# A graph network on one core: gathers and scatters of the GpSimd queue without waits for tiles and links

## The reference

```
h = max(layernorm(x), 0);  x = x + L0(h, src, dst)
h = max(layernorm(x), 0);  x = x + L1(h, edge_index, theta)
h = max(layernorm(x), 0);  x = x + L2(h, ..., edge_type)
h = max(layernorm(x), 0);  x = x + L3(h, src, dst)

# L2, for each edge e with x = h[src], y = h[dst]:
c      = w_comp[etype]                            # 16 coefficients
msg    = sum over b of c[b] * (x @ weight[b])     # 16 bases of 32 x 32
x_hat  = x @ A1_w.T + A1_b
y_hat  = y @ A2_w.T + A2_b + rel_emb[etype]
a      = tanh(relu(sum(x_hat * y_hat) / sqrt(32)))
h_new  = relu(segment_sum(a * msg, dst) + self-loop)  # where a node receives

# L3:
repeat 10 times: h = 0.9 * norm * segment_sum((norm * h)[src], dst) + 0.1 * feat
```

## Time and profile before

| | |
|---|---|
| median of 3 runs | 2976.82 us (2969.91 to 2977.31) |
| the profiled execution's own time | 2974.17 us |
| its span, first to last instruction | 2972.4 us |
| granted clock of TensorE | 1.00 throughout |
| busy: POOL, DVE, PE, ACT | 66%, 58%, 14%, 11% |

### The profile page before, as it was taken

The page is one execution under the profiler, slowest core; times in us unless marked ns, Lnnn a source line. Parts: engine busy times, 40 slices in busy tenths (PEclk is TensorE's granted clock), DMA queues, the critical chain, the costliest instruction groups (busy, mean ns, idle before and its releaser), DMA issues.

```text
span 2972.4 us, 14542 instructions
## 1 busy us (share of the span) xinstructions
PE 410.3 (14%) x2009; PEld 196.7 (7%) x2009; DVE 1735.8 (58%) x2999; ACT 329.6 (11%) x1032; POOL 1951.7 (66%) x1883
## 2 busy tenths in 40 slices
PE   0000000000000000000000039806870000015000
PEld 0000000000000000000000013302320000015000
DVE  8998885666786768112866658867789311431000
ACT  0000021111001110000111024403430000000000
POOL 6576777775456770577777755473668777466776
DMA  1001022221011310101210100000001100010000
GB/s 19 14 11 25 15 58 48 47 48 26 25 41 25 133 25 17 40 11 41 48 43 20 27 9 6 2 3 5 7 7 56 57 9 8 5 42 9 8 8 5
DMA packets 71098, 78.34 MB, mean 26 GB/s; under 512 B 38122, under 2 KB 63944, under 8 KB 69752
## 3 DMA queue, kind: packets, MB, share of 16 engines
q0 software_dynamic: 59456, 23.50, 6.0%
q1 hardware_dynamic: 5720, 28.67, 2.5%
q10 hardware_dynamic: 5856, 25.60, 2.3%
HBM read 36.82 MB, written 48.69 MB: 29 GB/s over the span
## 4 chain that ended last, share of the span: by engine, by line
DVE 41%; issue 27%; POOL 15%; PE 6%; another core or an unknown queue 4%; DVEq 2%; DMA 2%; ACT 1%; POOLq 0%; ACTq 0%; SPq 0%
POOL out L1525 10%; DVE mf L491 7%; DVE pay L491 4%; DVE z L491 3%; DVE psum L888 3%; POOL xs L1519 2%; DVE psum L494 2%; DVE mf L875 2%; PE psum L1941 2%; DVE mf L870 2%; PE psum L1942 1%; DVE outs L491 1%; POOL mf L1519 1%; DVE st L515 1%
## 5 line engine op out<-in xcount | busy, mean ns | idle before, releaser
L1525 POOL DMA_INDIRECT out<-outs,i_outS x196 | 224.8, 1147 | 130.8 <-DVE z L1338 73.1
L1519 POOL DMA_INDIRECT xs<-in_x,i_src x196 | 217.2, 1108 | 134.4 <-issue 54.8
L1519 POOL DMA_INDIRECT xd<-in_x,i_dst x196 | 208.5, 1064 | 108.3 <-DVE mf L491 44.6
L1519 POOL DMA_INDIRECT xd<-x_rows,i_dstX x196 | 205.7, 1050 | 106.6 <-issue 49.8
L1519 POOL DMA_INDIRECT mf<-x_rows,i_srcX x196 | 209.1, 1067 | 95.3 <-issue 60.0
L1525 POOL DMA_INDIRECT out<-outs,i_srcX x196 | 198.9, 1015 | 71.9 <-issue 61.5
L1519 POOL DMA_INDIRECT pay<-payload_by_dst,i_rank x196 | 195.6, 998 | 62.6 <-issue 62.6
L491 DVE TENSOR_TENSOR mf<-mf 128x128 f32<-128x128 f32 (+5 forms) x577 | 175.0, 341 | 14.0 <-DVE mf L491 3.5
L491 DVE TENSOR_TENSOR pay<-psum,pay 128x512 f32<-128x512 f32 x196 | 133.4, 688 | 85.2 <-ACT pay L1826 68.4
L1519 POOL DMA_INDIRECT mf<-l_own_rows,lists x124 | 123.8, 998 | 49.7 <-issue 37.4
L1519 POOL DMA_INDIRECT mf<-l_first_rows,lists x124 | 125.2, 1010 | 37.7 <-issue 37.7
(11 more groups left out here) (465 smaller groups left out, 2384.2 us busy)
## 6 DMA issues: line engine op xcount, KB each, us to landing
z<-in_x ACTq DMA_DIRECT2D x16, 624.0 KB
out<-z ACTq DMA_DIRECT2D x16, 624.0 KB
l_first_rows<-mf SPq DMA_DIRECT2D x2, 3234.0 KB, 9.6
l_own_rows<-pay SPq DMA_DIRECT2D x1, 3626.0 KB
payload_by_dst<-z SPq DMA_DIRECT2D x1, 3234.0 KB
x_rows<-z SPq DMA_DIRECT2D x1, 3234.0 KB
xd<-in_x,i_dst POOLq DMA_INDIRECT x196
xs<-in_x,i_src POOLq DMA_INDIRECT x196
```

Source lines behind the costliest of these rows:

```text
L1519: G.indirect_dma_start(out=dest(k), out_offset=None, in_=table, in_offset=bass.IndirectOffsetOnAxis(ap=idx[:, k:k + 1], axis=0), bounds_ch ...
L1525: G.indirect_dma_start(out=table, out_offset=bass.IndirectOffsetOnAxis(ap=idx[:, k:k + 1], axis=0), in_=source(k), in_offset=None, bounds_ ...
```

## The change

The waits for tiles (`l2_done`) and for links (`dve`) are removed from the gathers of part 1 and from the sends, with their three constants. Part 1's gathers are now issued one behind the other, right behind those of part 0; the sends are issued behind them, and wait only for `outs_ready` (and, once, for the dense rows, which were there long before). The order of the instructions stays; no other engine's program changes.

```diff
-ROWS_FREE, ROWS_BESIDE = 60, 84
-SENDS_BESIDE = 108
...
             for part, (lo, hi) in enumerate(L2_PARTS):
-                for dest, idx, landed in ((lambda k: XY[:, k, 0:X2W], "srcX", "x2src_in"), (lambda k: XDW[:, k, :], "dstX", "x2dst_in")):
-                    for k in range(lo, hi):
-                        if part == 1:
-                            if ROWS_FREE <= issued < ROWS_FREE + ROWS_BESIDE:
-                                pool.wait_ge(s["l2_done"], 2 + issued - ROWS_FREE)
-                            elif issued >= ROWS_FREE + ROWS_BESIDE:
-                                links_done = 5 * (issued - ROWS_FREE - ROWS_BESIDE + 1) // 2
-                                pool.wait_ge(s["dve"], min(marks["ends"] + links_done, marks["ended"]))
-                            issued += 1
-                        gather(dest, x2_dram, icols[idx], P * EC - 1, s[f"{landed}{part}"], 1, k)
+                gather(lambda k: XY[:, k, 0:X2W], x2_dram, icols["srcX"], P * EC - 1, s[f"x2src_in{part}"], hi - lo, lo)
+                gather(lambda k: XDW[:, k, :], x2_dram, icols["dstX"], P * EC - 1, s[f"x2dst_in{part}"], hi - lo, lo)
...
             for part, (lo, hi) in enumerate(L2_PARTS):
                 pool.wait_ge(s["outs_ready"], part + 1)
-                for k in range(lo, hi):
-                    if k < SENDS_BESIDE:
-                        pool.wait_ge(s["l2_done"], 2 + tiles_before + k * 10 // 11)
-                    scatter(out, lambda q: OUT[:, q, :], icols["outS"], N - 1, s["outs_scattered"], 1, k)
+                scatter(out, lambda q: OUT[:, q, :], icols["outS"], N - 1, s["outs_scattered"], hi - lo, lo)
```

More of the change, by code:

```diff
@@ L1609, in _ @@
             pool.wait_ge(s["s_final"], 1)
-            tiles_before = 4 * L2_TURNS[1][0]
-            issued = 0
             for part, (lo, hi) in enumerate(L2_PARTS):
-                for dest, idx, landed in ((lambda k: XY[:, k, 0:X2W], "srcX", "x2src_in"), (lambda k: XDW[:, k, :], "dstX", "x2dst_in")):
-                    for k in range(lo, hi):
-                        if part == 1:
-                            if ROWS_FREE <= issued < ROWS_FREE + ROWS_BESIDE:
-                                pool.wait_ge(s["l2_done"], 2 + issued - ROWS_FREE)
-                            elif issued >= ROWS_FREE + ROWS_BESIDE:
-                                links_done = 5 * (issued - ROWS_FREE - ROWS_BESIDE + 1) // 2
-                                pool.wait_ge(s["dve"], min(marks["ends"] + links_done, marks["ended"]))
-                            issued += 1
-                        gather(dest, x2_dram, icols[idx], P * EC - 1, s[f"{landed}{part}"], 1, k)
-            assert ROWS_BESIDE <= tiles_before
+                gather(lambda k: XY[:, k, 0:X2W], x2_dram, icols["srcX"], P * EC - 1, s[f"x2src_in{part}"], hi - lo, lo)
+                gather(lambda k: XDW[:, k, :], x2_dram, icols["dstX"], P * EC - 1, s[f"x2dst_in{part}"], hi - lo, lo)
             pool.wait_ge(s["dense_out"], 16 * (DCHUNKS + 1))
```

## The result

| | before | changed |
|---|---|---|
| median | 2977.07 us (2969.91 to 2979.01, 4 runs) | 3269.28 us (3255.8 to 3271.24, 4 runs) |
| ratio | | 1.0985, 95% interval 1.0958 to 1.1011 |
| span of the profiled execution | 2972.4 us | 3259.4 us |

The sign was forecast, the size was not: 3017.5 us was predicted, with a range up to 3122. Later on, the same two kernels were measured together again, in a set of runs in which the kernel before took 2755 us, and there the changed kernel was *faster*. That is told under the experiments, and it belongs to the result.

A forecast was written before the change was run, and what follows sets the result against it. POOL's backlog of sends was taken to bound the end. At 2.77 us a tile own rows shift +114.4 us, less 73.7 recovered: +40.7 on the profiled 2974.2, 3014.9, plus 2.6 to the median: 3017.5 us; range 2935 to 3122.

The forecast's parts named there:

- What bounds the kernel, and what goes: Between 2276 and 2520 POOL's backlog of sends counts; own rows, ready about 2287, are gathered 73.7 us later.
- R: Shift of the moment own rows are ready, against 2275.9; the end moves by R - 73.7 us; likeliest R +114.4.
- p: Time of one tile in L2's batches beside POOL's unpaced issues; forecast 2.77 us, break-even 2.45.
- p = 1.79: Tiles keep full pace beside continuous issues: batch 1 ends 1929, batch 2 2205; R = -14.9, change -89 us.
- The chain from p to the end: From p follow the ends of batch 1, `outs_ready` 2, sends and batch 2, then R; at 2.77 change +40.7 us.
- the crawl: PE's completions queue behind POOL's issues, never catching up: p 4 and above, +126 at 4, +161 at 5; chance 0.16.
- the sum settles only near 14: Tile time beside continuous issue, charging 1.25 us for each issue above one a tile, repeated: 2.26, 2.7, above 3, near 14.
- 7.16 + 3.91 = 11.07 a turn: Four tiles beside continuous issues take 7.16 us plus the 3.91 us stall of a seven-issue burst, every turn: p = 2.77.
- the high end: Upper bound for p: batch 1's first tiles beside 60 free gathers, two tiles from 1735.68 to 1760.36, 12 us each.
- +213 at 8: Upper limit of the crawl: at p = 8 us a tile the change would cost up to +213 us.
- Q: One server for POOL's issues (1.27 us) and tiles (0.52 us): tile takes 0.52 / (1 - 1.27 / T) at spacing T.
- L: Beside back-to-back issues one PE instruction passes per 1.40 us; pauses release everything held; a burst's first issues do no harm.

The follow-up runs named there:

- the pause behind every issue: Changed kernel with one one-column memset, and a wait for it, behind each gather of part 1 and each send: 3075.88 us; with six memsets 3377.05 us.
- the runs meant to tell it: Changed kernel with a one-memset pause behind only every fourth issue (2746.52 us, again 2748.09 and 2749.48) or every second (2805.58, again 2799.82); kernel before 2754.71 us.

## Why the prediction was wrong

**What bounds the kernel, and what goes.** Right. With the sends off the end, own rows are gathered 10.9 us after they are ready (10.8 by the sum), L3 follows them at a fixed distance (+4.9 us), and the end moved by R - 73.7: 356.0 - 73.7 = +282.3, measured +282.1 at the first gather. Where turns stayed at 7.16 us, in the later set, a gain did come, 64.5 us of the 89 that p = 1.79 had.

**The chain from p to the end.** Right as a form. With 22.4 in place of 2.77 the same steps give batch 1 an end of 2190 (2218 measured: the third product came at 1774.9 and not at 1760.4, POOL's sends lasted 5 us longer, and full pace returned only 27 us behind them), and a change of +269 for +287. Two terms in it were small and wrong: the lists were to be untouched, and are 17 us shorter without gathers beside them; and the crawl was to begin and end with POOL's issues, while in batch 2 some five tiles passed before it set in, and in batch 1 it outlasted them.

**The size of p.** This is the step that failed: 2.77 us a tile was forecast, 22.4 was measured. I had a sum in the text that comes near it and didn't follow it. Ten extra issues had cost 12.5 us, 1.25 us each, and with that price "the sum settles only near 14". By that sum p = 0.54 + p x 1.25 / 1.30: POOL takes nearly all of the time, and what is left over goes to a tile. With 1.27 in place of 1.25, within what that price was known to, it is 22. (With the price so near to the spacing the sum can be made to give almost any large p, so the 22.4 us don't prove it.) I took instead "7.16 + 3.91 = 11.07 a turn": one stall per turn, read from a burst of seven issues that stood between pauses. A burst pays its debt in the pause behind it; a stream has none. That the delay builds up and drains, the second batch of the changed kernel shows (five tiles before it sets in) and the end of its first sends (27 us until it is gone). I had also put aside the high end, 12 us a tile from the earlier trace rows, as "a start that no turn repeats". Without free gathers ahead of it that start was gone (the pause behind every issue), so it was the stretch of batch 1 that stood nearest to the changed kernel.

**The crawl.** Its mechanism was right in kind, its bound was not: the "+213 at 8" rested on no row that ends p there. The range ended at p = 4.5, while the sum above said 14. The chance of 0.16 was for the case that my own sum had.

**The rule of the Trainium skill.** The page "SBUF — State Buffer", section "Who interferes with whom", says "PE and ACT never wait on anyone". As a rule on SBUF's ports it is not contradicted: PE's instructions are not longer (0.60 and 0.30 us). What it doesn't cover is PE's reports, held here for 14 and 20 us. Whoever reads it as "POOL can't slow PE" is off by 290 us in one set of runs, and right in another.

**What stays open.** It is open what the shared thing is, and whether POOL's issuing or the transfers' traffic loads it. It is open whether it goes by mean rate (Q) or by bursts (L), since the runs meant to tell it fell where nothing is held. And it is open what makes the difference of 2980 and 2755 us. It is not the kernel; nor the granted clock, since both groups hold executions at a mean of 0.70 and of 1.00; nor a lasting property of a chip, if the record's numbers name chips: chip 2 has a set of either kind.

The profile does tell the two apart. In the ten traces of the 2980 us sets the page has no landing time for the gathers of the first rows, and in the ten of the 2755 us sets it has one. The changed kernel, first in the result, then when it was run again:

```profile
xs<-in_x,i_src POOLq DMA_INDIRECT x196
...
xs<-in_x,i_src POOLq DMA_INDIRECT x196, 2.4
```

## What to carry to other kernels

Where an extra unit of load costs nearly as much as its own spacing (1.25 of 1.30 us), don't add up stalls: solve for the steady state, and if it is far off, believe it. Read a change that takes pauses away from the stretch without pauses, however short it is, not from bursts between pauses. Where a pace of waits looks needed, try room between the issues as well: here a spacing of 1.88 us kept the tiles free as the waits for tiles did, though it cost POOL more time than there was (3076 us). And before such a change is kept or dropped, measure both kernels side by side in more than one set of runs: here it cost nearly 10% in one and gained 2.4% in another.

## What the runs showed of the hardware

- Beside indirect transfers issued every 1.30 us by GpSimd, TensorE's semaphore increments came 14 and 20 us late (0.01 us in the kernel before), and a tile took 22.4 us with 8 matmuls and 8 weight loads, 14.0 us with 5 and 5: 1.40 us for each of both, or 2.80 us for each matmul. Increments of ScalarE to TensorE came within 0.1 us in the same stretch. Spaced 1.88 us apart, the same transfers held nothing; nor did some 590 small memsets of GpSimd in 160 us.
- The delay builds up and drains: after a pause of 223 us in the transfers it set in about five tiles into the batch, and behind the last transfer of another stretch it took 27 us to go (2050.2 to 2077).
- In three of six sets of runs the effect was absent: the same kernel took 2755 us in place of 2980, and the changed one 2690 in place of 3269. The sign of this change depends on it. The traces with the effect hold fewer than 60% of the semaphore events of those without.
